# Gate logits read from PSUM, and the second layer norm moved to GpSimd, in a fused attention and mixture-of-experts kernel

## Chip, cores and metric

The kernel runs on one core of a Trainium2 chip. The metric is the device time of one execution in microseconds (us); lower is better. The median of three executions before the change is 131.92 us.

## The reference, cut to what matters

2048 tokens of width 128 go through one attention block and one mixture of 8 experts, each on layer-normed input and with a residual:

```python
x = x + attention(ctx, layernorm(x), Wq)          # causal, sequences of 64, keys = values = ctx @ Wq.T
xf = layernorm(x)
gates = softmax(xf @ gate_W)                       # 8 experts
tk_g, tk_i = top_k(gates, 2);  tk_g = tk_g / (sum(tk_g) + 1e-8)
cw = sum(one_hot(tk_i) * tk_g)
out = xf
for e in range(8):                                 # every expert is computed for every token
    out += cw[:, e] * (relu(xf @ W1[e] + b1[e]) @ W2[e] + b2[e])
x = x + out
```

## The kernel before, in words

The 2048 tokens are 16 tiles of 128, taken in 4 groups of 4 tiles (`TG = 4`, `GROUPS = 4`), numbered 0 to 3. The code is written engine by engine, each with its own order of instructions and waits on counting semaphores; nothing is scheduled automatically. The attention and the gate of group 0, and half of the attention of group 1, are a prologue. After it each group is a loop over 8 experts, and each expert has two slots (even and odd, 16 per group) into which the attention, second norm and gate of the *next* group (or the one after) are put, by the tables `steps` of each engine.

Per expert e, TensorE first does `hidden_product(g, e + 1)` (6 products of 512 columns in fp16: hi times hi, hi times lo, lo times hi, for two halves c = 0 and 1 of the 256 hidden units), then the even slot, then `output_product(g, e)`, then the odd slot. ScalarE turns each half in PSUM into `h_hi` (fp16, L570) and `h` (fp32, L571). For a "split" expert the low part `h_lo = h - h_hi` is also needed: half c = 0 is computed on GpSimd (`hidden_lo0`, L690) and half c = 1 on VectorE (`hidden_lo`, L848). The output product of a split expert multiplies `h_hi` first and ends with 8 products on `h_lo`, before which it waits for both halves. Experts 0 and 3 (0 and 7 in group 3) are not split and run in fp32. VectorE adds each expert's output into `acc` (`add_expert`, L864, four instructions per expert), in the order `hidden_lo(g, e + 1)`, even slot, `add_expert(g, e)`, odd slot.

The second norm of the next group: VectorE makes mean and variance (slot 5), GpSimd the reciprocal root by a power (L673, slot 5), VectorE writes `xf` in four instructions (`second_norm`, L784, slot 7), TensorE transposes `xf` (L292, slot 10), ScalarE makes `x_hi` (L548) and VectorE `x_lo` (L790, slot 10), and TensorE makes the gate's logits in PSUM (L354 to L356, slot 12). GpSimd also adds `x1 + xf` into `acc` (`base_sum`, L682, slot 10). VectorE then picks the top two experts (`gate_top`, slot 13, whose result `below` ScalarE exponentiates at L553 before it goes on to the next group's first hidden layer), `gate_choice` (slot 14) and `gate_weights` (slot 15). The weights in fp16 halves are transposed by TensorE for the b2 term.

In group 0 the loop also holds the conversion of the last two pairs of expert weights (L951, L957 on VectorE). `chain.link` makes VectorE wait for the instruction just issued.

Of the kernel before, what the change touches and what calls it, by code (L numbers as in the profile page):

```python
# [5 lines left out]
fp16 = mybir.dt.float16  # L6
i32 = mybir.dt.int32
ALU = mybir.AluOpType
ACT = mybir.ActivationFunctionType
AX = mybir.AxisListType  # L10
# [23 lines left out]
def xattn_moe(nc, x, ctx, wq, gate_w, w1, b1, w2, b2, out):  # L34
    P = 128
# [11 lines left out]
    SX, SW, SH = 16.0, 64.0, 16.0  # L47
    FULL = (0, 3)
    FULL_LAST = (0, 7)
    HB = 2 * C  # L50
    Y_FREE = 2
    SK, SV = 4.0, 64.0
# [10 lines left out]
    def is_split(g, e):  # L63
        return e not in (FULL_LAST if isinstance(g, int) and g == GROUPS - 1 else FULL)

    def splits(g, e):

        return g * (E - len(FULL)) + sum(is_split(g, i) for i in range(e + 1))

    stack = ExitStack()  # L70
    with stack:  # L71
        def sb(name, shape, dt=fp32):
            return stack.enter_context(nc.sbuf_tensor(name, shape, dt))
# [61 lines left out]
        rstd2 = sb("rstd2", [P, TG])  # L135
        xf = sb("xf", [P, TG, D])

        logits = sb("logits", [P, TG, E])
        top8 = sb("top8", [P, TG, 8])
        below = sb("below", [P, TG, E])  # L140
        gate_exp = sb("gate_exp", [P, TG, E])
        is_second = sb("is_second", [P, TG, E])
        nth = sb("nth", [P, TG, E])
        one_above = sb("one_above", [P, TG])
        above = sb("above", [P, TG, E])
        chosen = sb("chosen", [P, TG, E])
        sum_two = sb("sum_two", [P, TG])
        sum_all = sb("sum_all", [P, TG])
        inv_two = sb("inv_two", [P, TG])
        weight = sb("weight", [P, TG, E])  # L150
        weight_y = sb("weight_y", [P, 2, TG, E])
        weight_cat = sb("weight_cat", [P, TG, NB2], fp16)
        weight_catT = sb("weight_catT", [NB2, TG, P], fp16)

        x_hi = sb("x_hi", [P, GROUPS, GT], fp16)
# [88 lines left out]
        def over(ap, n):  # L244

            return ap.unsqueeze(2).broadcast_to([P, TG, n])
# [40 lines left out]
        def _(pe):  # L287
# [73 lines left out]
            def cat_transposes(g):  # L361
                pe.wait_ge(cat_ready, g + 1)
                for t in range(TG):
                    last = nc.tensor.transpose(cat_ps[:, t, :], weight_cat[:, t, :], ident16[:, :])
                last.then_inc(catT_ps, 1)

            def b2_product(g):
# [22 lines left out]
            def output_product(g, e):  # L390

                n = g * E + e
                i = e % 2
                split = is_split(g, e)
                if split:
                    pe.wait_ge(w2lo_ready, e // 2 + 1)
                else:
                    pe.wait_ge(w2_in[e // 2], 16)
                pe.wait_ge(h_ready, (n + 1) * C)
                pe.wait_ge(y_used, n + 1)  # L400
                last_expert = n_is_last(g, e)

                def add_product(t, hidden, weights, start, stop):


                    o = LAST_BANKS[t][:, 0:D] if last_expert else tiles(psY[i])[:, t, :]
                    for c in range(C):
                        last = nc.tensor.matmul(o, hidden[:, C * i + c, t * P:(t + 1) * P], weights[:, e, c, :],  # L408
                                                start=start and c == 0, stop=stop and c == C - 1)
                    if stop and (last_expert or t == TG - 1):  # L410
                        last.then_inc(y_ps, 1)

                for t in range(TG):
                    if split:
                        add_product(t, h_hi, w2_hi, last_expert or t == 0, False)
                        add_product(t, h_hi, w2_lo, False, False)
                    else:
                        add_product(t, h, w2_sb, True, True)
                if split:
                    pe.wait_ge(hlo_ready, splits(g, e))  # L420
                    pe.wait_ge(hlo0_ready, splits(g, e))
                    for t in range(TG):
                        add_product(t, h_lo, w2_hi, False, last_expert or t == TG - 1)

# [93 lines left out]
        def _(act):  # L518
# [31 lines left out]

            def gate_exps(a):
                act.wait_ge(below_ready, a + 1)
                nc.scalar.activation(gate_exp[:, :, :], below[:, :, :], ACT.Exp).then_inc(gate_exp_ready, 1)  # L553

            cat_ps = psD[0:NB2, 0:TG * P // 2].bitcast(fp16).rearrange("p (t n) -> p t n", n=P)

# [90 lines left out]
        def _(pool):  # L647
# [22 lines left out]
            def attention_rstd(a, ts):  # L670
                v = slice(ts[0], ts[-1] + 1)
                pool.wait_ge(var2_ready, a * TG + ts[-1] + 1)
                nc.gpsimd.tensor_tensor(rstd2[:, v], var2[:, v], half[:, v], ALU.pow).then_inc(rstd2_ready, len(ts))  # L673
# [10 lines left out]

            def hidden_lo0(g, e):

                if is_split(g, e):
                    i = C * (e % 2)
                    pool.wait_ge(h_ready, (g * E + e) * C + 1)
                    nc.gpsimd.tensor_tensor(h_lo[:, i, :], h[:, i, :], h_hi[:, i, :],  # L690
                                            ALU.subtract).then_inc(hlo0_ready, 1)

            steps = [(FIRST_RSTD, 2, first_rstd), (RSTD, 1, lambda a: attention_rstd(a, ALL)), (BASE, 1, base_sum)]

            def group(g):
                for e in range(E):
# [28 lines left out]
        def _(dve):  # L725
# [71 lines left out]
            def gate_top(a, chain):  # L797

                dve.wait_ge(logits_ps, a + 1)
                chain.link(nc.vector.tensor_scalar(logits[:, :, :], psD[:, 0:TG * E].rearrange("p (t e) -> p t e", e=E),  # L800
                                                   1.0 / (SX * SW), None, ALU.mult))
                for t in range(TG):
                    last = nc.vector.max(top8[:, t, :], logits[:, t, :])
                chain.link(last)
                TT(below[:, :, :], logits[:, :, :], over(first, E), ALU.subtract).then_inc(below_ready, 1)
                TT(is_second[:, :, :], logits[:, :, :], over(second, E), ALU.is_equal)
                TT(one_above[:, :], first, second, ALU.is_gt)
                chain.link(TT(above[:, :, :], logits[:, :, :], over(second, E), ALU.is_gt))

            def gate_choice(a, chain, meanwhile):  # L810

# [10 lines left out]

            def gate_weights(a, chain):
                dve.wait_ge(gate_exp_ready, a + 1)
                chain.link(TT(chosen[:, :, :], chosen[:, :, :], gate_exp[:, :, :], ALU.mult))
                nc.vector.reduce_sum(sum_two[:, :], chosen[:, :, :], axis=AX.X)
                chain.link(nc.vector.reduce_sum(sum_all[:, :], gate_exp[:, :, :], axis=AX.X))
                chain.link(nc.vector.scalar_tensor_tensor(out=sum_two[:, :], in0=sum_all[:, :], scalar=1e-8,
                                                          in1=sum_two[:, :], op0=ALU.mult, op1=ALU.add))
                chain.link(nc.vector.reciprocal(inv_two[:, :], sum_two[:, :]))  # L830
                chain.link(TT(weight[:, :, :], chosen[:, :, :], over(inv_two[:, :], E), ALU.mult))
                if a >= 2:
                    dve.wait_ge(y_used, Y_FREE + (a - 1) * E)
                if a >= 1:
                    dve.wait_ge(catT_ps, a)
                nc.vector.tensor_scalar(weight_y[:, a % 2, :, :], weight[:, :, :], 1.0 / (SH * SW), None, ALU.mult)
                nc.vector.tensor_scalar(weight_cat[:, :, 64:64 + E], weight[:, :, :], SX, None, ALU.mult)
                chain.link(nc.vector.tensor_scalar(weight_cat[:, :, 0:E], weight[:, :, :], SX, None, ALU.mult))
                nc.vector.scalar_tensor_tensor(out=weight_cat[:, :, 32:32 + E], in0=weight[:, :, :], scalar=SX,
                                               in1=weight_cat[:, :, 0:E], op0=ALU.mult,  # L840
                                               op1=ALU.subtract).then_inc(cat_ready, 1)
                dve.wait_ge(cat_ready, a + 1)

            def hidden_lo(g, e):
                if is_split(g, e):
                    i = C * (e % 2) + 1
                    dve.wait_ge(h_ready, (g * E + e + 1) * C)
                    nc.vector.tensor_tensor(h_lo[:, i, :], h[:, i, :], h_hi[:, i, :],  # L848
                                            ALU.subtract).then_inc(hlo_ready, 1)
# [48 lines left out]
            def wq_lo_part():  # L898
                dve.wait_ge(wq_hi_ready, 2)
                for whole, hi, lo in ((gram, gram_hi, gram_lo), (wqT, wqT_hi, wqT_lo)):  # L900
# [1 line left out]
                                                   op0=ALU.mult, op1=ALU.subtract).then_inc(wq_lo_ready, 1)  # L902

            steps = [(CTX_LO, 2, ctx_lo_part), (STATS, 2, statistics), (MAX, 2, lambda a: mask_and_max(a, ALL, banks_of(a))),
                     (RESIDUAL, 1, residual_step), (VARIANCE, 1, variance_step), (NORM2, 1, lambda a: second_norm(a, ALL)),
                     (X_LO, 1, lambda a: x_lo_part(a, ALL, LOOP_BANKS)), (GATE_TOP, 1, lambda a: gate_top(a, chain)),
                     (CHOICE, 1, choice_step), (WEIGHTS, 1, lambda a: gate_weights(a, chain))]

# [124 lines left out]
```

## Time and profile before

| | |
|---|---|
| times of three executions | 131.65, 131.92, 132.03 us; median 131.92 |
| profiled execution | 130.83 us, of it span 129.0 us from the first to the last instruction |
| TensorE (PE) busy | 120.3 us, 93% of the span |
| VectorE (DVE) busy | 107.6 us, 83% |
| ScalarE (ACT) busy | 93.5 us, 73% |
| GpSimd (POOL) busy | 53.5 us, 41% |
| granted TensorE clock | 1.000 |

Busy time is the union of the instructions' intervals. Matmuls overlap in the pipeline, so the time between the starts of two of them tells more than their durations: a 128x512 fp16 product has a duration of 379 ns, but the next one starts 0.216 us after it.

### The profile page before, as it was taken

The numbers are of one execution on the slowest core, as the hardware profiler recorded it, in microseconds if no ns is written. First come the engines' busy times: TensorE is split into PE (matmuls) and PEld (weight loads), VectorE is DVE, ScalarE is ACT, GpSimd is POOL, SyncE is SP. The second block draws the span as 40 slices with busy tenths as digits, with TensorE's granted clock in tenths as the row PEclk, the third lists the DMA queues.
The fourth block names the chain that finished last, engine by engine and source line by source line (L and its number), as shares of the span: only waits on it lengthen the run. The fifth ranks groups of instructions, "written<-read, shape, count | busy, mean of one in ns | idle before, by whom it ended". The sixth has DMA issues, their size and how long they took to land. (4 is left out here: it accounts for less than half of the span.)

```text
span 129.0 us, 3295 instructions
## 1 busy us (share of the span) xinstructions
PE 120.3 (93%) x1175; PEld 90.7 (70%) x1175; DVE 107.6 (83%) x419; ACT 93.5 (73%) x191; POOL 53.5 (41%) x57
## 2 busy tenths in 40 slices
PE   6987788999979999999999999999999979999991
PEld 2585566777847768778768778778776757776690
DVE  0629998989999999989898999958998798866683
ACT  3337485999776955996779927993799467989830
POOL 7199155330094951330095640330468303345400
PEclk9999999999999999999999999999999999999999
DMA  3999900000000000200000000200000002000002
GB/s 92 321 283 321 289 26 8 0 0 0 5 0 0 0 5 3 81 0 5 0 0 5 0 3 13 68 5 0 3 0 8 0 0 86 3 0 0 5 0 81
DMA packets 9904, 5.54 MB, mean 43 GB/s; under 512 B 504, under 2 KB 9888, under 8 KB 9888
## 3 DMA queue, kind: packets, MB, share of 16 engines
q1 hardware_dynamic: 9744, 5.27, 15.2%
q8 instruction: 9, 0.15, 0.5%
q10 hardware_dynamic: 144, 0.07, 0.2%
q14 instruction: 7, 0.06, 0.1%
HBM read 4.28 MB, written 1.05 MB: 41 GB/s over the span
## 5 line engine op out<-in xcount | busy, mean ns | idle before, releaser
L690 POOL TENSOR_TENSOR h_lo<-h,h_hi 128x512 f16<-128x512 f32 x24 | 28.7, 1196 | 40.2 <-ACT h L571 39.9
L571 ACT ACTIVATE h<-psH,b1T 128x512 f32<-128x512 f32 x64 | 43.3, 689 | 1.1 <-PE psH L508 0.9
L570 ACT ACTIVATE h_hi<-psH,b1T 128x512 f16<-128x512 f32 x48 | 33.0, 688 | 11.5 <-PE psH L387 11.4
L864 DVE SCALAR_TENSOR_TENSOR acc<-psY,weight_y,acc 128x128 f32<-128x128 f32 x125 | 35.1, 342 | 1.4 <-PE psY L408 1.2
L383 PE MATMUL psH<-x_hi,w_hi 128*128 128x512 f16 x62 | 23.5, 379 | 1.0 <-ACT h L571 1.0
L387 PE MATMUL psH<-x_lo,w_hi 128*128 128x512 f16 x62 | 23.5, 379 | 0.0
L384 PE MATMUL psH<-x_hi,w_lo 128*128 128x512 f16 x62 | 23.5, 379 | 0.0
L848 DVE TENSOR_TENSOR h_lo<-h,h_hi 128x512 f16<-128x512 f32 x24 | 16.5, 689 | 7.8 <-ACT h L571 7.3
L408 PE MATMUL psY<-w_hi,h_hi 128*128 128x128 f16 x192 | 22.7, 219 | 0.0
L408 PE MATMUL psY<-w_lo,h_hi 128*128 128x128 f16 x192 | 22.7, 219 | 0.0
L408 PEld LDWEIGHTS psY<-w_hi,h_hi 128*128 128x128 f16 x192 | 15.3, 98 | 2.2
L408 PE MATMUL psY<-w_hi,h_lo 128*128 128x128 f16 x192 | 14.6, 219 | 0.8 <-POOL h_lo L690 0.8
L408 PEld LDWEIGHTS psY<-w_sb,h 128*128 128x128 f32 x116 | 14.1, 192 | 1.0
L408 PEld LDWEIGHTS psY<-w_lo,h_hi 128*128 128x128 f16 x192 | 14.7, 98 | 0.0
L408 PE MATMUL psY<-w_sb,h 128*128 128x128 f32 x116 | 14.3, 275 | 0.0
L673 POOL TENSOR_TENSOR rstd<-var,half 128x4 f32<-128x4 f32 (+1 forms) x5 | 4.7, 953 | 21.8 <-DVE var L771 21.8
L408 PEld LDWEIGHTS psY<-w_hi,h_lo 128*128 128x128 f16 x192 | 11.6, 98 | 1.0 <-issue 0.9
L387 PEld LDWEIGHTS psH<-x_lo,w_hi 128*128 128x128 f16 x62 | 6.1, 98 | 7.3
L383 PEld LDWEIGHTS psH<-x_hi,w_hi 128*128 128x128 f16 x62 | 6.1, 98 | 6.9 <-ACT h L571 3.1
L384 PEld LDWEIGHTS psH<-x_hi,w_lo 128*128 128x128 f16 x62 | 6.1, 98 | 2.8
L677 POOL TENSOR_TENSOR rstd<-mv,half 128x4 f32<-128x4 f32 x4 | 5.0, 1250 | 5.8 <-DVE mv L734 5.8
L682 POOL TENSOR_TENSOR acc<-x,xf 128x512 f32<-128x512 f32 x4 | 7.1, 1784 | 0.0
(191 smaller groups left out, 191.4 us busy)
## 6 DMA issues: line engine op xcount, KB each, us to landing
w_sb<-in_L_ffn_W_dram SPq DMA_DIRECT2D x8, 256.0 KB, 4.9
out_dram<-acc SPq DMA_DIRECT2D x3, 256.0 KB, 2.3
x_sb<-in_x_dram SPq DMA_DIRECT2D x2, 256.0 KB, 4.0
ctx_sb<-in_ctx_dram SPq DMA_DIRECT2D x2, 256.0 KB, 4.4
x_sb<-in_x_dram SPq DMA_DIRECT2D x1, 512.0 KB, 7.6
ctx_sb<-in_ctx_dram SPq DMA_DIRECT2D x1, 512.0 KB, 8.5
out_dram<-acc SPq DMA_DIRECT2D x2, 128.0 KB, 1.8
wq_sb<-in_L_xattn_Wq_dram ACTq DMA_DIRECT2D x1, 64.0 KB, 2.8
```

The source lines that it names most:

```text
L383: nc.tensor.matmul(psH[c][:, :], w1_hi[:, e, w], x_hi[:, g, :], start=True, stop=False)
L384: nc.tensor.matmul(psH[c][:, :], w1_lo[:, e, w], x_hi[:, g, :], start=False, stop=False)
L387: nc.tensor.matmul(psH[c][:, :], w1_hi[:, e, w], x_lo[:, g, :], start=False, stop=True).then_inc(z_ps, 1)
L408: last = nc.tensor.matmul(o, hidden[:, C * i + c, t * P:(t + 1) * P], weights[:, e, c, :], start=start and c == 0, stop=stop and c == C - 1)
L570: nc.scalar.activation(h_hi[:, C * (e % 2) + c, :], psH[c][:, :], ACT.Relu, bias=bias, scale=scale)
L571: nc.scalar.activation(h[:, C * (e % 2) + c, :], psH[c][:, :], ACT.Relu, bias=bias, scale=scale).then_inc(h_ready, 1)
L673: nc.gpsimd.tensor_tensor(rstd2[:, v], var2[:, v], half[:, v], ALU.pow).then_inc(rstd2_ready, len(ts))
L677: nc.gpsimd.tensor_tensor(rstd[:, bass.ts(a, TG)], mv[:, bass.ts(a, TG), 1], half[:, 0:TG], ALU.pow).then_inc(rstd_ready, TG)
L682: nc.gpsimd.tensor_tensor(acc[:, bass.ts(a, TG), :], x1[:, :, :], xf[:, :, :], ALU.add).then_inc(base_ready, 1)
L690: nc.gpsimd.tensor_tensor(h_lo[:, i, :], h[:, i, :], h_hi[:, i, :], ALU.subtract).then_inc(hlo0_ready, 1)
L848: nc.vector.tensor_tensor(h_lo[:, i, :], h[:, i, :], h_hi[:, i, :], ALU.subtract).then_inc(hlo_ready, 1)
L864: last = nc.vector.scalar_tensor_tensor(out=o, in0=y, scalar=weight_y[:, g % 2, t, e:e + 1], in1=o, op0=ALU.mult, op1=ALU.add)
```

## The change

Three things are changed at once. (1) In the gate, the copy of the logits from PSUM to SBUF with the factor 1/1024 is gone; the gate's comparisons read PSUM, and the factor goes into ScalarE's exponential. The two sums are one instruction on a doubled tile, the normalised weight and its scaled copy are one, and two of the fp16 writes are one. (2) `xf` of groups 1 to 3 is written by GpSimd (`loop_norm`) instead of VectorE, at the same slot 7. (3) For expert 4 of groups 0 to 2, both halves of `h_lo` are computed on VectorE, and GpSimd skips it (`pool_takes`).

```diff
+    DVE_PAIR = 4
+    def pool_takes(g, e):
+        return is_split(g, e) and not (e == DVE_PAIR and g < GROUPS - 1)
...
-        weight_cat = sb("weight_cat", [P, TG, NB2], fp16)
+        weight_cat = sb("weight_cat", [P, TG, P], fp16)
...
                     pe.wait_ge(hlo_ready, splits(g, e))
-                    pe.wait_ge(hlo0_ready, splits(g, e))
+                    pe.wait_ge(hlo0_ready, pool_splits(g, e))
...
-                nc.scalar.activation(gate_exp[:, :, :], below[:, :, :], ACT.Exp).then_inc(gate_exp_ready, 1)
+                nc.scalar.activation(picked[:, 1, :, :], below[:, :, :], ACT.Exp,
+                                     scale=1.0 / (SX * SW)).then_inc(gate_exp_ready, 1)
...
             def hidden_lo0(g, e):
-                if is_split(g, e):
+                if pool_takes(g, e):
...
+            def loop_norm(a):
+                pool.wait_ge(rstd2_ready, (a + 1) * TG)
+                for t in range(TG):
+                    nc.gpsimd.tensor_scalar(xf[:, t, :], x1[:, t, :], mv2[:, t, 0:1], rstd2[:, t:t + 1],
+                                            ALU.subtract, ALU.mult).then_inc(xf_ready, 1)
+
-            steps = [(FIRST_RSTD, 2, first_rstd), (RSTD, 1, lambda a: attention_rstd(a, ALL)), (BASE, 1, base_sum)]
+            steps = [(FIRST_RSTD, 2, first_rstd), (RSTD, 1, lambda a: attention_rstd(a, ALL)), (NORM2, 1, loop_norm),
+                     (BASE, 1, base_sum)]
...
                 dve.wait_ge(logits_ps, a + 1)
-                chain.link(nc.vector.tensor_scalar(logits[:, :, :], psD[:, 0:TG * E].rearrange("p (t e) -> p t e", e=E),
-                                                   1.0 / (SX * SW), None, ALU.mult))
+                logits = psD[:, 0:TG * E].rearrange("p (t e) -> p t e", e=E)
...
-                chain.link(TT(chosen[:, :, :], chosen[:, :, :], gate_exp[:, :, :], ALU.mult))
-                nc.vector.reduce_sum(sum_two[:, :], chosen[:, :, :], axis=AX.X)
-                chain.link(nc.vector.reduce_sum(sum_all[:, :], gate_exp[:, :, :], axis=AX.X))
+                chain.link(TT(picked[:, 0, :, :], chosen[:, :, :], picked[:, 1, :, :], ALU.mult))
+                chain.link(nc.vector.reduce_sum(sums[:, :, :], picked[:, :, :, :], axis=AX.X))
...
-                chain.link(TT(weight[:, :, :], chosen[:, :, :], over(inv_two[:, :], E), ALU.mult))
+                w = weight_y[:, a % 2, :, :]
+                chain.link(nc.vector.scalar_tensor_tensor(out=w, in0=picked[:, 0, :, :], scalar=1.0 / (SH * SW),
+                                                          in1=over(inv_two[:, :], E), op0=ALU.mult, op1=ALU.mult))
...
-                nc.vector.tensor_scalar(weight_y[:, a % 2, :, :], weight[:, :, :], 1.0 / (SH * SW), None, ALU.mult)
-                nc.vector.tensor_scalar(weight_cat[:, :, 64:64 + E], weight[:, :, :], SX, None, ALU.mult)
-                chain.link(nc.vector.tensor_scalar(weight_cat[:, :, 0:E], weight[:, :, :], SX, None, ALU.mult))
+                parts = weight_cat[:, :, :].rearrange("p t (q n) -> p t q n", n=P // 2)
+                chain.link(nc.vector.tensor_scalar(parts[:, :, :, 0:E], w.unsqueeze(2).broadcast_to([P, TG, 2, E]),
+                                                   SX * SH * SW, None, ALU.mult))
...
             def hidden_lo(g, e):
+                if is_split(g, e) and not pool_takes(g, e):
+                    i = C * (e % 2)
+                    dve.wait_ge(h_ready, (g * E + e) * C + 1)
+                    nc.vector.tensor_tensor(h_lo[:, i, :], h[:, i, :], h_hi[:, i, :], ALU.subtract)
...
-                     (RESIDUAL, 1, residual_step), (VARIANCE, 1, variance_step), (NORM2, 1, lambda a: second_norm(a, ALL)),
+                     (RESIDUAL, 1, residual_step), (VARIANCE, 1, variance_step), 
```

The prologue's `xf` of group 0 stays on VectorE.

## Rows read from the trace of the kernel before

**Rows 1.** The page: busy time by engine, and the granted TensorE clock in 40 slices.

```profile
PE 120.3 (93%) x1175; PEld 90.7 (70%) x1175; DVE 107.6 (83%) x419; ACT 93.5 (73%) x191; POOL 53.5 (41%) x57
...
PEclk9999999999999999999999999999999999999999
```

**Rows 2.** Timeline of TensorE: start, duration (us), line, operation, count, idle time before.

```profile
25.84 1.13 PE L292 MATMUL psB<-ident,probs 128*128 128x128 f32 x4
26.81 0.28 PE L408 MATMUL psY<-w_hi,h_hi 128*128 128x128 f16 x2
...
37.67 0.28 PE L408 MATMUL psY<-w_lo,h_hi 128*128 128x128 f16 x2
38.69 0.61 PE L408 MATMUL psY<-w_hi,h_lo 128*128 128x128 f16 x8 [0.75 <-POOL h_lo L690]
...
40.43 0.60 PE L292 MATMUL psB<-ident,xf 128*128 128x128 f32 x4
...
99.59 0.18 PE L354 MATMUL psD<-gate_hi,x_hi 128*128 128x8 f16 x1
...
104.76 0.38 PE L383 MATMUL psH<-x_hi,w_hi 128*128 128x512 f16 x1 [0.72 <-ACT h L571]
```

**Rows 3.** Timeline of ScalarE around the gate's exponential, prologue and group 2.

```profile
22.53 0.23 ACT L553 ACTIVATE gate_exp<-below 128x32 f32<-128x32 f32 x1 [0.63 <-DVE below L805]
22.67 0.67 ACT L570 ACTIVATE h_hi<-psH,b1T 128x512 f16<-128x512 f32 x1
...
103.81 0.23 ACT L553 ACTIVATE gate_exp<-below 128x32 f32<-128x32 f32 x1 [2.53 <-DVE below L805]
```

**Rows 4.** Timeline of VectorE: the gate's instructions, prologue and group 1.

```profile
21.68 0.18 DVE L800 TENSOR_SCALAR logits<-psD 128x32 f32<-128x32 f32 x1
21.90 0.37 DVE L803 MAX8 top<-logits 128x8 f32<-128x8 f32 x4
...
54.40 0.19 DVE L826 TENSOR_REDUCE sum_two<-chosen 128x4 f32<-128x32 f32 x1
54.50 0.17 DVE L827 TENSOR_REDUCE sum_all<-gate_exp 128x4 f32<-128x32 f32 x1
...
55.34 0.18 DVE L836 TENSOR_SCALAR weight_y<-weight 128x32 f32<-128x32 f32 x1
...
55.73 0.19 DVE L839 SCALAR_TENSOR_TENSOR weight_cat<-weight,weight_cat 128x32 f16<-128x32 f32 x1
```

**Rows 5.** Timeline of VectorE and GpSimd in group 0 around expert 4.

```profile
36.84 0.69 DVE L848 TENSOR_TENSOR h_lo<-h,h_hi 128x512 f16<-128x512 f32 x1
...
38.49 2.02 DVE L784 TENSOR_SCALAR xf<-x,mv,rstd 128x128 f32<-128x128 f32 x4
...
35.76 1.32 POOL L673 TENSOR_TENSOR rstd<-var,half 128x4 f32<-128x4 f32 x1 [6.78 <-DVE var L771]
37.06 2.60 POOL L690 TENSOR_TENSOR h_lo<-h,h_hi 128x512 f16<-128x512 f32 x2
```

**Rows 6.** Timeline: VectorE instructions that arrive while GpSimd is busy.

```profile
9.97 1.50 POOL L706 TENSOR_SCALAR w_hi<-w_sb 128x512 f16<-128x512 f32 x1
...
10.60 0.69 DVE L951 SCALAR_TENSOR_TENSOR w_lo<-w_sb,w_hi 128x512 f16<-128x512 f32 x1
...
23.99 1.20 POOL L690 TENSOR_TENSOR h_lo<-h,h_hi 128x512 f16<-128x512 f32 x1 [2.90 <-ACT h L571]
24.21 1.03 DVE L825 TENSOR_TENSOR chosen<-chosen,gate_exp 128x32 f32<-128x32 f32 x1
```

**Rows 7.** Timeline of GpSimd and VectorE in group 2 around the base sum.

```profile
98.24 1.83 POOL L682 TENSOR_TENSOR acc<-x,xf 128x512 f32<-128x512 f32 x1
...
98.24 0.69 DVE L848 TENSOR_TENSOR h_lo<-h,h_hi 128x512 f16<-128x512 f32 x1 [0.37 <-ACT h L571]
```

**Rows 8.** Groups of instructions by form: count, busy us, mean ns of one, idle before.

```profile
L957 DVE SCALAR_TENSOR_TENSOR w_lo<-w_sb,w_hi 128x512 f16<-128x512 f32 x4 | 2.7, 678 | 0.0
...
L790 DVE SCALAR_TENSOR_TENSOR x_lo<-psB,x_hi 128x512 f16<-128x512 f32 x3 | 2.0, 683 | 0.0
```

More of the change, by code:

```diff
@@ L68, in splits, with pool_splits @@
         return g * (E - len(FULL)) + sum(is_split(g, i) for i in range(e + 1))
+    def pool_takes(g, e):
+        return is_split(g, e) and not (e == DVE_PAIR and g < GROUPS - 1)
+    def pool_splits(g, e):
+        return sum(pool_takes(j, i) for j in range(g) for i in range(E)) + sum(pool_takes(g, i) for i in range(e + 1))
     stack = ExitStack()
@@ L136, in xattn_moe @@
         xf = sb("xf", [P, TG, D])
-        logits = sb("logits", [P, TG, E])
         top8 = sb("top8", [P, TG, 8])
         below = sb("below", [P, TG, E])
-        gate_exp = sb("gate_exp", [P, TG, E])
+        picked = sb("picked", [P, 2, TG, E])
         is_second = sb("is_second", [P, TG, E])
@@ L146, in xattn_moe @@
         chosen = sb("chosen", [P, TG, E])
+        sums = sb("sums", [P, 2, TG])
         sum_two = sb("sum_two", [P, TG])
-        sum_all = sb("sum_all", [P, TG])
         inv_two = sb("inv_two", [P, TG])
-        weight = sb("weight", [P, TG, E])
         weight_y = sb("weight_y", [P, 2, TG, E])
-        weight_cat = sb("weight_cat", [P, TG, NB2], fp16)
+        weight_cat = sb("weight_cat", [P, TG, P], fp16)
         weight_catT = sb("weight_catT", [NB2, TG, P], fp16)
@@ L363, in cat_transposes @@
                 for t in range(TG):
-                    last = nc.tensor.transpose(cat_ps[:, t, :], weight_cat[:, t, :], ident16[:, :])
+                    last = nc.tensor.transpose(cat_ps[:, t, :], weight_cat[:, t, 0:NB2], ident16[:, :])
                 last.then_inc(catT_ps, 1)
@@ L804, in gate_top @@
                 chain.link(last)
-                TT(below[:, :, :], logits[:, :, :], over(first, E), ALU.subtract).then_inc(below_ready, 1)
-                TT(is_second[:, :, :], logits[:, :, :], over(second, E), ALU.is_equal)
+                TT(below[:, :, :], logits, over(first, E), ALU.subtract).then_inc(below_ready, 1)
+                TT(is_second[:, :, :], logits, over(second, E), ALU.is_equal)
                 TT(one_above[:, :], first, second, ALU.is_gt)
-                chain.link(TT(above[:, :, :], logits[:, :, :], over(second, E), ALU.is_gt))
+                chain.link(TT(above[:, :, :], logits, over(second, E), ALU.is_gt))
             def gate_choice(a, chain, meanwhile):
@@ L824, in gate_weights @@
                 dve.wait_ge(gate_exp_ready, a + 1)
-                chain.link(TT(chosen[:, :, :], chosen[:, :, :], gate_exp[:, :, :], ALU.mult))
-                nc.vector.reduce_sum(sum_two[:, :], chosen[:, :, :], axis=AX.X)
-                chain.link(nc.vector.reduce_sum(sum_all[:, :], gate_exp[:, :, :], axis=AX.X))
-                chain.link(nc.vector.scalar_tensor_tensor(out=sum_two[:, :], in0=sum_all[:, :], scalar=1e-8,
-                                                          in1=sum_two[:, :], op0=ALU.mult, op1=ALU.add))
+                chain.link(TT(picked[:, 0, :, :], chosen[:, :, :], picked[:, 1, :, :], ALU.mult))
@@ L830, in gate_weights @@
+                chain.link(nc.vector.reduce_sum(sums[:, :, :], picked[:, :, :, :], axis=AX.X))
+                chain.link(nc.vector.scalar_tensor_tensor(out=sum_two[:, :], in0=sums[:, 1, :], scalar=1e-8,
+                                                          in1=sums[:, 0, :], op0=ALU.mult, op1=ALU.add))
                 chain.link(nc.vector.reciprocal(inv_two[:, :], sum_two[:, :]))
-                chain.link(TT(weight[:, :, :], chosen[:, :, :], over(inv_two[:, :], E), ALU.mult))
                 if a >= 2:
@@ L837, in gate_weights @@
-                nc.vector.tensor_scalar(weight_cat[:, :, 64:64 + E], weight[:, :, :], SX, None, ALU.mult)
-                chain.link(nc.vector.tensor_scalar(weight_cat[:, :, 0:E], weight[:, :, :], SX, None, ALU.mult))
-                nc.vector.scalar_tensor_tensor(out=weight_cat[:, :, 32:32 + E], in0=weight[:, :, :], scalar=SX,
+                parts = weight_cat[:, :, :].rearrange("p t (q n) -> p t q n", n=P // 2)
+                chain.link(nc.vector.tensor_scalar(parts[:, :, :, 0:E], w.unsqueeze(2).broadcast_to([P, TG, 2, E]),
+                                                   SX * SH * SW, None, ALU.mult))
@@ L840, in gate_weights @@
+                nc.vector.scalar_tensor_tensor(out=weight_cat[:, :, 32:32 + E], in0=w, scalar=SX * SH * SW,
                                                in1=weight_cat[:, :, 0:E], op0=ALU.mult,
```

## The prediction

> **What bounds the kernel now.** I read the page first: TensorE is busy 93% of the span at the full granted clock, 2.4 GHz, in all 40 slices [rows 1]. So the question is only which gaps of TensorE the change closes or opens. The timeline of TensorE answers it. From 40.43 to 99.1 us the starts follow each other at the products' own pace (0.216 us per 512-column product), apart from two gaps of 0.14 us behind the softmax. In that stretch a faster VectorE buys nothing, but a late operand costs its whole lateness. The gaps of the loop, each found as the distance between two starts less the pace of the work between them, are: 0.48 us before 26.81 (four transposes from 25.84 need 4 x 0.12; they wait for the softmax on ScalarE), 0.3 us before 30.9 (transposed weights on ScalarE), 0.91 us before 38.69 (last weight load group at 37.67 plus 0.11; waits for GpSimd's `h_lo` of expert 4), 0.29 us before 99.59 (logits wait for `x_lo`) and 0.90 us before 104.76 (waits for ScalarE's `h`) [rows 2]. They sum to about 2.9 us, and this is all that edits of the loop can win.
>
> Then I asked what ends each wait. ScalarE runs its exponential of the gate in order ahead of the hidden layer, and idles for VectorE's `below` 0.63 us in the prologue and 2.53 us at the end of group 2 [rows 3]. In group 2 that is what makes `h` late for 104.76. In the prologue ScalarE goes from 22.67 without idling through the softmax that TensorE waits for before 26.81.
>
> **The gate, in the prologue and per group.** By my count four instructions per group go: the logits copy, one reduction, one of the two weight products and one fp16 write. The copy and its link cost the distance from 21.68 to 21.90, 0.22 us [rows 4]. The merged reduction saves 0.10 us (54.40 to 54.50). From L836 to L839 the chain takes 0.39 us (55.34 to 55.73); one linked step of that kind takes 0.21 to 0.22, so 0.17 is saved. Two instructions get 64 elements per partition instead of 32, some 0.03 us each. Together 0.10 + 0.17 - 0.06 = 0.21 us, and with the copy 0.43 us of VectorE per group. Only the 0.22 of the copy lies ahead of `below`; the rest hides in VectorE's own idle time before the next `h_lo`, which waits for ScalarE.
> What reading PSUM costs: the 128x512 operation takes 683 ns with an input in PSUM (L790) and 678 from SBUF (L957) [rows 8], so I take 0; the other bound is that those 5 ns are paid by each of 7 reading instructions, 0.035 us.
> The Trainium skill (VectorE: DVE Perf Modes, section on the TRN2 errata) gives a VectorE instruction 58 fixed cycles from SBUF and 120 from PSUM. By it two chained steps ahead of `below` would give back about 0.13 of the 0.22 us, an estimate from that page; the trace's pair of rows disagrees at 5 ns.
>
> *On TensorE's path:* in the prologue `below`, the exponential at 22.53, ScalarE's unbroken row and the last transposes all come 0.22 us earlier: -0.22 before 26.81, and still so at 30.9 and 37.6. At the end of group 2 `below` again comes 0.22 earlier: -0.22 before 104.76. At the ends of groups 0 and 1 keys, values and scores keep TensorE supplied: 0.
>
> **Expert 4's half on VectorE.** Before, GpSimd starts it at 37.06, because the power for the norm (35.76, 1.32 us) is queued ahead, and TensorE gets it at 38.69 [rows 2, 5]. After, VectorE starts at 36.84 - 0.22 = 36.62, does the two halves 0.61 apart, and the second ends near 37.92; with 0.1 us to TensorE the `h_lo` products start near 38.0. TensorE would like them at 37.78 - 0.22 = 37.56. So TensorE is at 38.0 instead of 38.69: -0.69 in all, of which -0.47 is new. In groups 1 and 2 this product had no gap, and needs its operand 1.1 us after VectorE's first half begins, which is near two halves of 0.61: 0, at worst +0.1 each. Behind the added instruction `add_expert` of expert 3 is queued, 0.61 us later; its PSUM bank is wanted again only for expert 5, over 2 us later: 0.
>
> **`xf` on GpSimd.** VectorE loses the four instructions, 2.02 us in group 0, in which the first stands about 0.9 us behind GpSimd's `h_lo` [rows 5]. Against the 0.61 it gains, VectorE is about 1.4 us lighter per group. GpSimd loses 1.16 to 1.3 us and gains the four. No GpSimd row has this form. The nearest is its one-operation tensor-scalar of 512 elements, 1.50 us [rows 6]: a quarter is 0.38, and I take 0.42 each with the start-up. The low bound is a quarter of the 1.20 us subtraction, 0.30; the high bound two operations at 0.38, 0.75. GpSimd starts them when the power ends, near 36.9 in group 0, and ends at 36.9 + 4 x 0.42 = 38.6 (39.9 at the high bound). TensorE wants the last transpose's operand at 40.43 - 0.69 + 0.36 = 40.1. It is hidden at both bounds. No DMA is issued by either queue in the loop, so none moves.
> The next in GpSimd's queue is `h_lo` of expert 5, then expert 6, then the base sum. Expert 5's half runs from 38.6 to 39.8 and is wanted at about 41.1: hidden, and at the high bound (39.9 + 1.2 = 41.1) just so.
>
> **Sum.** -0.22 - 0.47 - 0.22 = -0.91 us, from 130.83 us of the profiled execution (span 129.0, 1.8 us around it) to 129.9. The three timed executions have their median at 131.92, 1.09 above the profiled one; I apply the difference to it: 131.0 us.
>
> **Rivals.**
> *A. The two engines block each other (slower).* A VectorE instruction with two operands in SBUF, arriving while GpSimd does a subtraction, stands until it ends: L825 takes 1.03 us instead of 0.18 [rows 6], and 38.49 shows VectorE standing through a second queued GpSimd instruction as well [rows 5]. After the change GpSimd has five instructions in a row (four `xf`, one `h_lo`) when VectorE arrives with `h_lo` of expert 5. In group 2 VectorE then arrives with `h_lo` of expert 6 later than the 98.24 at which it and the base sum now start together [rows 7]. If the base sum gets there first, VectorE waits 1.2 us more; `x_lo` and the logits at 99.59, which have no slack, follow by 1.2 us. Group 1 has about 0.6 us of slack more (the input transposes), so +0.6; group 0 loses about 0.7. With the gate's 0.44 kept: +0.7 + 0.6 + 1.2 - 0.91 = +1.6 us, 133.5. It decides when VectorE is free of expert 4's sum later than 98.24; if `xf` may not start during VectorE's two halves, I work that out as 96.66 + 4 r, which for r = 0.42 is 98.3. Against it: GpSimd's tensor-scalar at 9.97 ran 1.50 us with VectorE's two-operand instruction inside it at 10.60, which took its normal 0.69 [rows 6]. So `xf` itself seems not to block, it ends before 95 in group 2, and VectorE is free some 0.6 us before 98.24. Chance 0.22.
> The Trainium skill (SBUF — State Buffer, "Who interferes with whom") states the full lock: a VectorE instruction with two SBUF inputs and a GpSimd one that reads SBUF exclude each other for the whole instruction. By that rule this rival would be the likeliest. Rows 6 bear it out for the subtraction and not for the tensor-scalar.
> *B. The gain of group 0 is eaten there.* Group 0 has the weight conversions as well, and VectorE has no idle time from 30 to 50 us. If it stands once more behind GpSimd (1.2 us at expert 5 or at the base sum), `x_lo` comes no earlier than before, TensorE waits at the logits and the 0.69 is lost: -0.22 remains, 131.7. For it: VectorE arrives at expert 5 near 38.9, in the middle of GpSimd's `h_lo`. Against: the removed `xf` stood 0.9 us, so one wait replaces another. Chance 0.28.
> *C. GpSimd's `xf` is far dearer than its bound*, 1.0 us each: it ends at 97.1 in group 2, TensorE waits at the transposes and again for expert 5, about 1 us in each of three groups less 0.91: 134.0. Nothing in the rows speaks for it. Chance 0.05.
>
> **Chances and range.** The sum above: 0.45. A measurement of this kernel tells about 0.3%, 0.4 us, from no change. The sum is faster; B is inside it; A and C are slower. Mixed outcomes between the sum and B, and between B and A, put some of each to its neighbour: faster 0.49, same 0.26, slower 0.25. The low end is the sum with VectorE's relief closing 0.4 us more of the gaps at 30.9, 38.0 and 99.59: 130.6. The high end reaches into A, when only group 2 or only group 1 pays: 132.9. The likeliest case alone spans 130.7 to 131.4.
>
> **What would show it.** After the change, the distance from the exponential's end to the softmax's transposes stays, and the first output product of expert 1 starts near 26.6; the `h_lo` products of expert 4 near 38.0; GpSimd's four `xf` last 1.6 to 1.8 us and no TensorE row waits for them; the row that was at 104.76 shows a wait of 0.5 instead of 0.72. I am wrong if VectorE's `h_lo` rows, all 0.69 now, show some of 1 to 2 us, and if the logits products show a wait for `x_lo` in groups 0 to 2.

## The result, and the profile after

The changed kernel takes 134.03 us (median of 4, 133.14 to 134.26) against 131.78 us (131.64 to 132.03): ratio 1.017, 95% interval 1.010 to 1.023. It is slower by 1.7%; the prediction was 131.0, with 132.9 as its high end. The profiled execution took 134.25 us with a span of 132.4.

Two views tell most of it. On the page, first the busy times and then the group of instructions that moved (line, operation, count, busy us, mean ns of one, idle before):

```profile
PE 122.6 (93%) x1175; PEld 91.8 (69%) x1175; DVE 105.8 (80%) x394; ACT 94.2 (71%) x191; POOL 60.7 (46%) x66
...
L702 POOL TENSOR_SCALAR xf<-x,mv,rstd 128x128 f32<-128x128 f32 x12 | 12.1, 1015 | 0.3
```

VectorE has 25 instructions less, 16 of them in the gate, and is less busy; TensorE is busy for the same share (93%) of a span that is 3.4 us longer. Twelve instructions that I had priced at 0.42 us stand with a mean of 1.015. The timeline of TensorE, in the places of [rows 2]:

```profile
27.10 0.93 PE L297 MATMUL psB<-ident,probs 128*128 128x128 f32 x4
27.87 0.28 PE L413 MATMUL psY<-w_hi,h_hi 128*128 128x128 f16 x2
...
38.73 0.28 PE L413 MATMUL psY<-w_lo,h_hi 128*128 128x128 f16 x2
39.26 0.62 PE L413 MATMUL psY<-w_hi,h_lo 128*128 128x128 f16 x8 [0.25 <-DVE h_lo L865]
...
41.01 0.38 PE L297 MATMUL psB<-ident,xf 128*128 128x128 f32 x2
42.16 0.33 PE L297 MATMUL psB<-ident,xf 128*128 128x128 f32 x1 [0.77 <-POOL xf L702]
42.94 0.33 PE L297 MATMUL psB<-ident,xf 128*128 128x128 f32 x1 [0.45 <-POOL xf L702]
...
99.25 0.49 PE L297 MATMUL psB<-ident,xf 128*128 128x128 f32 x3
100.01 0.33 PE L297 MATMUL psB<-ident,xf 128*128 128x128 f32 x1 [0.27 <-ACT h L577]
...
103.40 0.18 PE L359 MATMUL psD<-gate_hi,x_hi 128*128 128x8 f16 x1 [0.27 <-DVE x_lo L803]
...
108.20 0.38 PE L388 MATMUL psH<-x_hi,w_hi 128*128 128x512 f16 x1 [0.36 <-ACT h L577]
```

Two things happened at once. The gaps that the change was to shrink did shrink, by about 0.20 us before 27.87, 0.49 before 39.26 and 0.37 before 108.20. And new gaps stand where there were none: in the four transposes of `xf` that ran without one from 40.43 [rows 2]. Counted between starts, which otherwise stand 0.11 us apart there, they are 0.93 and 0.67 us in group 0 and 0.44 and 0.43 in groups 1 and 2. The row at 100.01 names ScalarE, but that engine had long been done; the last `xf` of GpSimd ends at 99.95, as the timeline of GpSimd and VectorE in group 2 shows:

```profile
95.65 0.69 DVE L861 TENSOR_TENSOR h_lo<-h,h_hi 128x512 f16<-128x512 f32 x1
96.26 0.69 DVE L865 TENSOR_TENSOR h_lo<-h,h_hi 128x512 f16<-128x512 f32 x1
...
98.57 0.71 DVE L865 TENSOR_TENSOR h_lo<-h,h_hi 128x512 f16<-128x512 f32 x1 [0.59 <-ACT h L577]
99.21 1.11 DVE L881 SCALAR_TENSOR_TENSOR acc<-psY,weight_y,acc 128x128 f32<-128x128 f32 x4
101.20 1.54 DVE L865 TENSOR_TENSOR h_lo<-h,h_hi 128x512 f16<-128x512 f32 x1 [0.88 <-ACT h L577]
...
95.12 1.01 POOL L679 TENSOR_TENSOR rstd<-var,half 128x4 f32<-128x4 f32 x1 [6.08 <-DVE var L784]
96.23 3.72 POOL L702 TENSOR_SCALAR xf<-x,mv,rstd 128x128 f32<-128x128 f32 x4
99.92 2.27 POOL L696 TENSOR_TENSOR h_lo<-h,h_hi 128x512 f16<-128x512 f32 x2
102.16 1.71 POOL L688 TENSOR_TENSOR acc<-x,xf 128x512 f32<-128x512 f32 x1
```

L861 and L865 are VectorE's two subtractions for a split expert: the half that it took over, and its own. The view of the `xf` tile gives the durations of GpSimd's instructions (ns, minimum/median/maximum):

```profile
L702 POOL TENSOR_SCALAR xf<-x,mv,rstd x12: 789/832/1541, 38.3 to 99.1; 128x128 f32<-128x128 f32 x12
```

One costs 0.79 us undisturbed. In groups 1 and 2 the first takes 1.31: here it was issued at 96.23, while VectorE's two subtractions of expert 4 ran until near 96.9. The four take 1.31, 0.79, 0.79 and 0.87 us, overlap by 0.01 each, and make up the 3.72 us of the row. TensorE wanted the last at 99.58. In group 0 two of the four are held up, 1.54 us each: the first, from 38.26, behind VectorE's pair of expert 4, and the third, from 40.57, behind VectorE's subtraction of expert 5 and L974 (the low half of an expert's weights, a conversion that group 0 alone holds), so that the four take 4.63 us. So the two parts of the change hit each other: the pair that was put on VectorE stands in front of the norm that was put on GpSimd.

**A second difference lies ahead of the loop.** The first 512-column product of the loop starts at 21.47 us before and at 22.73 after. I use the stretch from it to the end of the span: 129.0 - 21.47 = 107.53 us before and 132.4 - 22.73 = 109.67 after, so the loop lost 2.14 us and the prologue 1.26. TensorE's timeline of the prologue, before:

```profile
5.18 0.38 PE L292 MATMUL psY<-ident,x_sb 128*128 128x128 f32 x2
5.40 0.39 PE L474 MATMUL psD<-wq_c,wq_sb 128*128 128x128 f32 x2
```

and after:

```profile
5.20 0.63 PE L297 MATMUL psH<-ident,x_sb 128*128 128x128 f32 x2
5.63 0.64 PE L297 MATMUL psY<-ident,x_sb 128*128 128x128 f32 x2
6.05 0.63 PE L479 MATMUL psD<-wq_c,wq_sb 128*128 128x128 f32 x2
6.48 0.63 PE L297 MATMUL psH<-ident,ctx_sb 128*128 128x128 f32 x2
```

The same pairs stand 0.22 us apart in one and 0.42 in the other, which is full and half pace, 2.4 and 1.2 GHz. The view of the granted clock reads 1.00 in both, but it has nothing to read there: the trace keeps that clock as periods with a start, the first one, at full clock, starts at 4.72 us before and at 7.09 us after, and ahead of it nothing is kept. Before these pairs TensorE did the same nine products on zeros in both. The changed kernel's execution keeps the half pace until about 7.1 us, which costs 1.04 us; the rest, 0.22, comes through VectorE's L968, the same kind of conversion, which arrived 0.06 us after a GpSimd tensor-scalar had started and took 1.10 us instead of 0.69. Nothing shows this to be the change's doing: in the experiments with nine products the first 512-column product comes at 21.62, 22.28 and 22.43 us without the norm's move (e1, e2, e4) and at 21.84 to 22.67 with it (e3, e5, e6, e9, e10).

### The profile page after: what moved, and what is told of

Same layout as the page of the kernel before. It is cut to its first block and busy times, and to the rows that moved or that the text cites. A ratio compares the mean times of both kernels' runs of the same rounds, so it can differ in the third digit from the quotient of the medians.

```text
span 132.4 us, 3281 instructions
## 1 busy us (share of the span) xinstructions
PE 122.6 (93%) x1175; PEld 91.8 (69%) x1175; DVE 105.8 (80%) x394; ACT 94.2 (71%) x191; POOL 60.7 (46%) x66
## 5 line engine op out<-in xcount | busy, mean ns | idle before, releaser
L696 POOL TENSOR_TENSOR h_lo<-h,h_hi 128x512 f16<-128x512 f32 x21 | 24.7, 1183 | 35.9 <-ACT h L577 35.9
L865 DVE TENSOR_TENSOR h_lo<-h,h_hi 128x512 f16<-128x512 f32 x24 | 19.2, 800 | 11.7 <-ACT h L577 11.4
L702 POOL TENSOR_SCALAR xf<-x,mv,rstd 128x128 f32<-128x128 f32 x12 | 12.1, 1015 | 0.3
```

The lines of the kernel that those rows point to most:

```text
L702: nc.gpsimd.tensor_scalar(xf[:, t, :], x1[:, t, :], mv2[:, t, 0:1], rstd2[:, t:t + 1], ALU.subtract, ALU.mult).then_inc(xf_ready, 1)
```

## The experiments

Each ratio is taken against executions of the kernel before on the same chip as the run (their medians lie between 131.33 and 131.77 us), so it can differ a little from the quotient of two times in the table. "Loop" is the stretch from the first 512-column product to the end of the span, in the one profiled execution.

| run | us | ratio to before, 95% | first product | loop us |
|---|---|---|---|---|
| before | 131.78 | 1 | 21.47 | 107.53 |
| changed kernel | 134.03 | 1.017 (1.010 to 1.023) | 22.73 | 109.67 |
| e1 gate alone | 130.54 | 0.995 (0.992 to 0.998) | 21.62 | 107.18 |
| e2 pair alone | 131.60 | 1.001 (0.998 to 1.005) | 22.28 | 107.42 |
| e3 norm alone | 136.16 | 1.034 (1.030 to 1.039) | 22.67 | 112.13 |
| e4 gate and pair | 130.30 | 0.992 (0.989 to 0.995) | 22.43 | 106.77 |
| e5 norm with one operation | 131.80 | 1.000 (0.997 to 1.003) | 22.02 | 107.98 |
| e6 norm split over both | 131.24 | 0.997 (0.994 to 1.000) | 22.20 | 107.30 |
| e7 as e4, 7 products ahead | 130.42 | 0.989 (0.986 to 0.992) | 21.78 | 106.82 |
| e8 as e4, 12 products | 131.58 | 0.997 (0.994 to 1.000) | 22.52 | 106.78 |
| e9 norm, two constants | 131.73 | 1.002 (0.999 to 1.005) | 21.86 | 108.04 |
| e10 norm, one operand | 132.09 | 1.006 (1.002 to 1.009) | 21.84 | 108.26 |
| e11 as e7, pair in group 0 alone | 130.41 | 0.991 (0.988 to 0.994) | 21.92 | 106.78 |
| e12 as e4, 5 products | 131.01 | 0.996 (0.993 to 1.000) | 22.71 | 106.79 |

### The three parts one by one: e1 to e4

e1 is the changed kernel with these two edits undone, e4 with the first alone undone, e2 as e4 with the gate of before, e3 with only the second undone and the gate of before:

```diff
-(VARIANCE, 1, variance_step), 
+(VARIANCE, 1, variance_step), (NORM2, 1, lambda a: second_norm(a, ALL)),     # and NORM2 out of GpSimd's steps
...
-        return is_split(g, e) and not (e == DVE_PAIR and g < GROUPS - 1)
+        return is_split(g, e)
```

Expected of the gate alone:

> Only the gate's edit, the norm on VectorE and expert 4's first half on GpSimd as before. My theory: TensorE gains 0.22 us ahead of the first output product of expert 1 and 0.22 us at the end of group 2, so 0.4 us less than before. Rival, that reading PSUM is dear or that VectorE's relief only shifts waits onto GpSimd: within 0.1 us of before.

Measured: 0.5% less, and a loop 0.35 us shorter; the gap ahead of the first output product of expert 1 is 0.32 instead of 0.52 us, that at the end of group 2 0.68 instead of 0.88. The theory holds.

> Only expert 4's two halves on VectorE, the norm stays on VectorE. My theory: the one gap of 0.91 us in group 0 shrinks to about 0.45, groups 1 and 2 unchanged: 0.4 to 0.5 us less than before. Rival, that 0.61 us more on VectorE in each group makes x_lo and the logits late: 0.2 us in group 0 and 0.3 in group 2 back, so no change.

Measured: the time can't be told from before; the loop is 0.11 us shorter. The theory's gap did fall from 0.91 to 0.42 us. Most of that comes back near where the rival put it: waits of 0.17 us at the logits of group 0 (`x_lo`) and 0.17 at the end of group 0, where there were none, and 0.93 instead of 0.88 at the end of group 2. So alone the pair pays with VectorE's time most of what it gains, and the rival was the nearer.

> Only the norm's four instructions on GpSimd, which still makes expert 4's half ahead of them. Theory from the trace after: each of the four takes 0.78 us of GpSimd, and the next h_lo stands behind them; in group 2 they end at 93.1 + 1.3 + 3.1 = 97.5 us against a need of 96.6, and expert 5's half at 98.7 against 97.6. So 1.1 us or more lost per group, 3 to 4.5 us over before. Rival, that the loss of the changed kernel comes from the pair: then this one is within 1 us of before.

Measured: 3.4% more, a loop 4.60 us longer. The rival is out: without the pair the move is worse, since expert 4's subtraction is then also in GpSimd's queue ahead of the norm. GpSimd in group 2:

```profile
97.48 1.26 POOL L697 TENSOR_TENSOR h_lo<-h,h_hi 128x512 f16<-128x512 f32 x1
98.73 3.36 POOL L703 TENSOR_SCALAR xf<-x,mv,rstd 128x128 f32<-128x128 f32 x4
102.06 2.72 POOL L697 TENSOR_TENSOR h_lo<-h,h_hi 128x512 f16<-128x512 f32 x2
```

> The changed kernel with the norm back on VectorE. Theory, that the move of the norm is the whole loss: the predicted sum without it, 0.7 to 0.9 us less than before, and 3 us less than the changed kernel. Rival, that the two edits undo each other or the first 20 us are longer with the new code: no better than before.

Measured: 0.8% less than before, a loop 0.76 us shorter than before and 2.90 shorter than the changed kernel's. The norm's move is the whole loss. Together the two edits gain more than the sum of each (0.35 and 0.11): the wait of 0.17 us that e2 has at the end of group 0 is gone in e4. I put that down to the VectorE time that the gate's edit frees. The wait of 0.16 at the logits of group 0 stays. The timelines of VectorE and GpSimd in group 0 show a gain that I had not counted:

```profile
38.82 1.12 DVE L880 SCALAR_TENSOR_TENSOR acc<-psY,weight_y,acc 128x128 f32<-128x128 f32 x4
39.85 1.10 DVE L796 TENSOR_SCALAR xf<-x,mv,rstd 128x128 f32<-128x128 f32 x4
...
38.54 1.37 POOL L696 TENSOR_TENSOR h_lo<-h,h_hi 128x512 f16<-128x512 f32 x1 [0.70 <-ACT h L577]
```

The four `xf` take 1.10 us on VectorE, not 2.02 [rows 5]: GpSimd has one subtraction there instead of two and is done when they begin. The long VectorE rows that made the move look worth its while were waits behind GpSimd. The pair alone removes them in group 0 and shortens them in groups 1 and 2, where one instruction of the four falls from 1.18 to 0.80 us.

### What one instruction costs on GpSimd: e5, e9, e10

```diff
-nc.gpsimd.tensor_scalar(xf[:, t, :], x1[:, t, :], mv2[:, t, 0:1], rstd2[:, t:t + 1], ALU.subtract, ALU.mult)
+nc.gpsimd.tensor_scalar(xf[:, t, :], x1[:, t, :], 1.0, None, ALU.mult)                    # e5
+nc.gpsimd.tensor_scalar(xf[:, t, :], x1[:, t, :], 0.25, 1.0, ALU.subtract, ALU.mult)      # e9
+nc.gpsimd.tensor_scalar(xf[:, t, :], x1[:, t, :], rstd2[:, t:t + 1], None, ALU.mult)      # e10
```

> The changed kernel, but GpSimd's four instructions multiply x1 by a constant (one operation, no per-partition operands): mean and variance are left out of xf, the rest of the computation stays. It prices the form. Theory 1, two operations cost twice one: each falls from about 0.78 us apart to about 0.40, TensorE's waits at the transposes go, and the time is 2 us less than the changed kernel. Theory 2, the form has a fixed cost or the second operation is free: 0.6 to 0.8 us as before and the same time.

> The changed kernel with GpSimd's four instructions doing two operations with constants, without per-partition operands (mean and variance are left out of xf). Theory, the second operation costs: one instruction again about 0.79 us where one operation took 0.53, and TensorE waits at the transposes of groups 1 and 2 as in the changed kernel. Rival, the per-partition operands cost: 0.53 and no such waits.

> The same with one operation and one per-partition operand (the mean is left out of xf). Theory, the second operation costs: 0.53 us. Rival, the operands cost: above 0.6 us.

The view of the `xf` tile, e5, then e9, then e10:

```profile
L702 POOL TENSOR_SCALAR xf<-x x12: 523/532/760, 37.5 to 96.1; 128x128 f32<-128x128 f32 x12
```

```profile
L702 POOL TENSOR_SCALAR xf<-x x12: 637/647/1057, 37.4 to 96.2; 128x128 f32<-128x128 f32 x12
```

```profile
L702 POOL TENSOR_SCALAR xf<-x,rstd x12: 597/597/1745, 37.4 to 96.8; 128x128 f32<-128x128 f32 x12
```

Neither theory of the price was right: the second operation and the operands each cost a part. (The time of e5 did fall by about the 2 us of its first theory, its loop by 1.69.) One operation with a constant takes 0.53 us, a second operation adds 0.115, a per-partition operand 0.065: 0.53 + 0.115 + 2 x 0.065 = 0.78, against the 0.79 measured. I had taken a quarter of the 512-element row of 1.50 us [rows 6]. With the 0.53 beside it, I estimate the elements at (1.50 - 0.53)/384 = 2.5 ns each and the instruction at 0.21 us before the first of them, so four instructions of 128 pay that start four times. It is an estimate from two lengths, and the longer row writes fp16 where the shorter writes fp32.

The operands have a second price. In groups 1 and 2 GpSimd's first `xf` starts just ahead of VectorE's second subtraction, while the first still runs, in all of these runs. Group 1 of e9, which has constants, and then of e10, which has one per-partition operand:

```profile
66.39 0.65 POOL L702 TENSOR_SCALAR xf<-x 128x128 f32<-128x128 f32 x1
...
66.43 0.80 DVE L865 TENSOR_TENSOR h_lo<-h,h_hi 128x512 f16<-128x512 f32 x1
```

```profile
66.68 1.12 POOL L702 TENSOR_SCALAR xf<-x,rstd 128x128 f32<-128x128 f32 x1
...
66.71 0.69 DVE L865 TENSOR_TENSOR h_lo<-h,h_hi 128x512 f16<-128x512 f32 x1
```

With constants the first `xf` is not held (0.65 us) and VectorE loses 0.1 us. With one operand it stands 0.52 us (1.12 instead of 0.60), the same 0.52 as in the changed kernel. So in groups 1 and 2 e5 and e9 took away most of the hold together with a part of the price.

In e5 and e9 no wait is left at the transposes of groups 1 and 2, and yet the loop is 0.45 and 0.51 us longer than before. The wait went elsewhere: VectorE in group 0 of e5, and GpSimd beside it:

```profile
40.19 1.64 DVE L974 SCALAR_TENSOR_TENSOR w_lo<-w_sb,w_hi 128x512 f16<-128x512 f32 x1
41.76 1.11 DVE L881 SCALAR_TENSOR_TENSOR acc<-psY,weight_y,acc 128x128 f32<-128x128 f32 x4
42.80 0.28 DVE L918 SCALAR_TENSOR_TENSOR gram_lo<-gram,gram_hi 128x128 f16<-128x128 f32 x1
42.99 1.35 DVE L918 SCALAR_TENSOR_TENSOR wqT_lo<-wqT,wqT_hi 128x128 f16<-128x128 f32 x1
...
39.94 2.93 POOL L696 TENSOR_TENSOR h_lo<-h,h_hi 128x512 f16<-128x512 f32 x2
42.82 1.38 POOL L688 TENSOR_TENSOR acc<-x,xf 128x512 f32<-128x512 f32 x1
```

VectorE's two-operand instructions stand 0.96 and 1.07 us behind GpSimd's subtractions and the base sum, `x_lo` is late, and TensorE waits 1.27 us at the logits of group 0. That is rival B of the prediction, by the blocking of rival A, in the place where it was put; it comes true when the norm on GpSimd is quick enough to bring the next subtractions forward. In e9 TensorE waits 0.24 us at the `h_lo` products of expert 5 and 0.96 at those logits. In e10 the transposes of group 0 still wait 0.73 and 0.47 us, and those of groups 1 and 2 not at all.

### Half of the norm on each engine: e6

```diff
-                for t in range(TG):        # GpSimd, loop_norm
+                for t in range(2, TG):     # and tiles 0 and 1 on VectorE at the same slot, a semaphore for each engine
```

> The changed kernel with two of the four norm instructions on VectorE and two on GpSimd. Theory, that the four in a row are what is late: GpSimd's end falls by 1.56 us, to 98.4 us in group 2 against a need near 99.6, so no wait at the transposes; total near that of the kernel with the norm wholly on VectorE, within 0.4 us. Rival, that the two engines' blocking is the cost: GpSimd's h_lo of expert 5 now starts when VectorE wants its own, which stands about 1 us, and each group loses 0.3 us or more at the h_lo products of expert 5: at least 0.8 us over that kernel.

Measured: 0.3% less than before, a loop 0.53 us over e4's, between the theory's 0.4 and the rival's 0.8. The transposes wait nowhere, as the theory said. Of the rival's waits one came, in group 0, where GpSimd's `h_lo` of expert 5 is held up instead of VectorE's:

```profile
40.07 4.40 POOL L700 TENSOR_TENSOR h_lo<-h,h_hi 128x512 f16<-128x512 f32 x2
```

Those two subtractions take 4.40 us (2.37 and 2.07) instead of 2.3, and TensorE waits 0.78 us. In groups 1 and 2 nothing was lost. So even half of the norm gains nothing on GpSimd.

### The first 22 us: e7, e8, e12

`WARM_UP` is the number of products on zeros that TensorE does ahead of its first real one.

```diff
-    WARM_UP = 9
+    WARM_UP = 7      # e7; 12 in e8, 5 in e12, each on e4
```

> Gate and pair without the move of the norm, with 7 instead of 9 products ahead of the kernel's work. Theory, that the executions differ by how long TensorE keeps half its pace in the first 7 us: with fewer products the first real ones come 0.4 to 0.9 us sooner when the wait for wq allows it, but more of them at half pace; the median moves by less than 0.5 us and the spread stays 1 us. Rival, that the spread is from the DMAs: the first wait for wq shows it.

> The same with 12 products. Theory: three more products at half pace end 1.3 us later, near 6.3 us, so real work starts later, at full pace: 0.3 to 1.3 us slower than with 9, with less spread. Rival, that the pace rises at a moment that the products don't set: then spread and median stay within 0.3 us.

> Gate and pair with 5 products ahead. Theory from the runs with 7, 9 and 12: the first real product can't start before wq at about 3.6 us, 7 end at 4.1, so two fewer save at most 0.5 us, and real products run at half pace longer; within 0.3 us of the version with 7.

Measured: with 5, 7, 9 and 12 products the ratios are 0.996, 0.989, 0.992 and 0.997, while the loops agree within 0.05 us. So the difference lies in the first 22 us. 7 and 9 can't be told apart in the ratios. That 5 would do as well as 7, and that 12 would narrow the spread, were expectations that fell: with 12 the executions spread over 1.18 us, with 9 over 1.26, with 5 over 1.71 (and one more at 132.38), with 7 over 0.43 in e7, where I had expected 1 us, but over 0.86 in e11, which starts the same way. The count does not by itself set when the pace rises. The trace's period of full clock starts at 4.72, 7.09, 3.88 and 6.95 us with nine products (before, changed, e1, e3), at 4.95 and 6.22 with seven (e7, e11), at 4.80 with twelve and at 8.26 with five, one profile each. In e12 TensorE waits for data after its five products and then does real work at half pace up to there; in e8 the twelve products are over at 5.55 and the real ones start late. That the DMA of wq sets the spread fell too: the first instruction that waits for it starts at 3.36 to 4.01 us in the profiles, and with nine products TensorE comes to its first product on wq at 4.45 or later. What decides when the pace rises stays open.

### Where the pair pays: e11

```diff
-        return is_split(g, e) and not (e == DVE_PAIR and g < GROUPS - 1)
+        return is_split(g, e) and not (e == DVE_PAIR and g == 0)
```

> Gate's edit, norm on VectorE, 7 products ahead, and expert 4's first half on VectorE in group 0 alone. Theory, only group 0 had a gap there: from the first loop product to the end within 0.1 us of the version with groups 0 to 2 (106.8 us), perhaps 0.05 less as the wait before the end of group 2 is 0.73 there and was 0.68 with the gate's edit alone. Rival, that VectorE's relief of GpSimd pays in groups 1 and 2 too: 0.2 us or more longer.

Measured: 106.78 us of loop against 106.82, a ratio of 0.991 against 0.989. In groups 1 and 2 the pair neither gains nor costs.

## Why the prediction was wrong, point by point

**What bounds the kernel: right.** TensorE without gaps from 40 to 99 us was the ground of the loss: an operand that comes 0.4 us late costs 0.4.

**The gate: right.** -0.22 and -0.22 were forecast, -0.20 and -0.20 measured in e1. Reading PSUM costs at most the 0.02 us between them. In the changed kernel the second term came out as -0.37, with 0.15 of it given back at the logits just before.

**Expert 4's pair: right in its place, too kind in its sum.** The gap fell by 0.49 us in the changed kernel, for 0.47 forecast. That the added VectorE time costs nothing holds nearly, and only with the gate's edit: e4's loop is 0.41 us shorter than e1's, while of the pair alone 0.11 us of the 0.49 stay.

**`xf` on GpSimd: the step that failed, twice.** I wrote "I take 0.42 each with the start-up", between 0.30 and 0.75; it measured 0.79, starts 0.78 apart. Scaling by elements left out what each instruction costs before its first element, 0.21 us by the estimate above, and the high bound doubled the scaled part alone, where the start, two operations and two operands add up. The second failure is "GpSimd starts them when the power ends, near 36.9": the first stood for VectorE's two subtractions, 0.75 us in group 0 and 0.52 in groups 1 and 2, and in group 0 the third stood for another 0.75. I had read that mechanism in [rows 7], where a base sum takes 1.83 us beside VectorE, and used it for VectorE's delays but not for GpSimd's in the main case. With both the sum for group 0 reads 38.26 + 2 x 0.75 + 4 x 0.78 = 42.9 us, where TensorE wanted the last at 41.01 + 3 x 0.11 = 41.34; "hidden at both bounds" was wrong in all three groups. The price alone would have cost next to nothing: without the holds the last `xf` ends near 38.26 + 4 x 0.78 = 41.4 in group 0 and 96.23 + 3.12 = 99.4 in group 2, wanted at 41.34 and 99.58. It took the dear instruction and the hold together; the wait behind VectorE is the term that the sum had put at nothing.

**The account of the loop.** New gaps 1.60 (transposes, group 0) + 0.87 (groups 1 and 2) + 0.48 (three of 0.16 at expert 5's `h_lo` products) + 0.15 (logits) = 3.10; gains 0.20 + 0.49 + 0.37 = 1.06; the difference is 2.04 of the measured 2.14 us.

**The rivals.** The nearest is rival C, a norm far dearer than its bound, to which I gave 0.05 with 134.0 us: 134.03 was measured. That the numbers agree is in part luck. C has 1.0 us per instruction by its own price and 1 us lost in each group; the runs show 0.79, only just over the bound of 0.75, the rest of the mean of 1.015 is standing behind VectorE, and the new gaps are 1.76 us in group 0, 0.59 in group 1 and 0.75 in group 2. That "Nothing in the rows speaks for it" was too strong: the page of before has GpSimd's power on 4 elements at 0.95 us each (L673), another operation, but a sign that a short instruction there isn't cheap by its elements. Rival A's blocking was real, and in both directions: `xf` is held behind VectorE's subtractions, and VectorE's `h_lo` of expert 6, the one that A named, takes 1.54 us (101.20), but behind GpSimd's own `h_lo` and not the base sum, and costs the logits of group 2 only 0.15.

By the prediction's own signs, the first output product of expert 1 and the `h_lo` products of expert 4 came on time (27.87 and 39.26, less the 1.26 us of the prologue, for 26.6 and 38.0), while the four `xf` lasted 3.7 to 4.6 us for 1.6 to 1.8, and VectorE shows `h_lo` rows of 1 to 2 us. GpSimd's tensor-scalar did not block VectorE's subtraction that came in the midst of it (0.71 us at 98.57), as [rows 6] said, but was itself held by it; L968 in the prologue, which came 0.06 us after the start of one, did lose 0.41 us.
The Trainium skill (SBUF — State Buffer, "Who interferes with whom") has the later of the two block for the whole instruction. It is near the 1.54 us of the first `xf` and the 1.64 of L974 in e5, and does not fit the 0.71 at 98.57.

**The base of the sum.** I set the gain against the profiled 130.83 and then added the distance from it to the median, 1.09 us, as if it were the same in every execution. Part of it is TensorE's half pace in the prologue, 0 to 1 us and different in each execution. It did not decide the outcome.

## What to carry to other kernels

Price a moved instruction on its new engine from two lengths of a near form, so that its fixed part shows, and multiply by the count; a quarter of a long row is a low bound. Then add what it stands behind the other engine: here, by the sums above, neither the price nor the hold alone would have made the transposes of groups 1 and 2 wait (with 0.42 each and the hold, the last `xf` would end at 96.23 + 0.52 + 1.68 = 98.4). An instruction that looks slow on one engine may be standing behind the other engine that you want to move it to: free that engine first (here by the pair) and look again. When both directions of a swap touch VectorE and GpSimd, draw both queues on one time line, with each two-operand instruction of VectorE as a possible wait for GpSimd's and the other way round.

Of the versions tried, the gate's edit with the pair and the norm left on VectorE beats both kernels: 0.992 (0.989 to 0.995) with nine products ahead and 0.989 (0.986 to 0.992) with seven.

## What the runs showed of the hardware that was not expected

GpSimd's tensor-scalar on 128x128 fp32 takes 0.53 us with one operation and a constant, 0.65 with two, 0.60 with one per-partition operand and 0.79 with two operations and two operands, where VectorE does the last in 0.275 us per instruction (four in 1.10). Started beside VectorE's subtraction in groups 1 and 2, it stands 0.52 us if it has a per-partition operand (changed kernel, e10), and at most 0.02 if it has constants (e5, e9); the instruction behind it then takes 0.72 us instead of 0.53 or 0.64. GpSimd's subtraction of 512 elements grows from 1.16 to as much as 2.37 us (e6) beside VectorE's two-operand instructions, and VectorE's two-operand instructions from 0.69 to 1.64 (e5) or 1.75 (e9) behind GpSimd's. The view of the granted clock reads 1.00 from 5 to 7 us, where the changed kernel's products start at half pace, because the trace keeps no clock ahead of its first period (7.09 us there, 4.72 before, and none at all in e2, e4 and e6); only the distance between starts shows the pace.
